# A fused feed-forward, attention and feed-forward kernel: the order of two transfers on SyncE, and four more multiplications of ones in one step of TensorE

## The reference

```python
x = x + 0.5 * ffn(layernorm(x))       # phase 0: 8 experts, capacity 512 slots each
x = x + attn(layernorm(x))            # 16 heads of 16, keys and queries normalized and rotated
x = x + 0.5 * ffn(layernorm(x))       # phase 1: 8 experts again
```

```python
scores = einsum('bhtd,bhsd->bhts', q, k) * scale + 1.0
attn = softmax(scores, axis=-1)
y = einsum('bhts,bhsd->bhtd', attn, v)
return y.reshape(B, T, C) @ wproj.T
```

## Time and profile before

| | us |
|---|---|
| three plain executions | 2152.18, 2154.19, 2148.09 |
| their median | 2152.18 |
| the profiled execution's own time | 2156.22 |
| its span, first to last instruction | 2154.3 |

### The profile page before, as it was taken

The page is one execution under the profiler, slowest core; times in us unless marked ns, Lnnn a source line. Parts: engine busy times, 40 slices in busy tenths (PEclk is TensorE's granted clock), DMA queues, the critical chain, the costliest instruction groups (busy, mean ns, idle before and its releaser), DMA issues.

```text
span 2154.3 us, 39634 instructions
## 1 busy us (share of the span) xinstructions
PE 2077.9 (96%) x14658; PEld 1073.5 (50%) x14658; DVE 1725.6 (80%) x2558; ACT 1684.0 (78%) x3255; POOL 987.9 (46%) x1221
## 2 busy tenths in 40 slices
PE   5799999999999999999999999999999999999997
PEld 4588975433444444444444444444444333236987
DVE  7776769988879888987988798888879889436774
ACT  5566647888888898988898898989888888755664
POOL 5786438652751672285067227614840201104542
PEclk9899999999999999999999999999999999899999
DMA  7454414345443444335433434435442425203331
GB/s 252 140 188 171 148 59 84 70 102 113 80 88 74 96 93 96 70 91 123 74 77 81 101 64 94 110 78 86 76 108 46 88 42 119 61 4 129 118 130 57
DMA packets 137857, 208.94 MB, mean 97 GB/s; under 512 B 30527, under 2 KB 95295, under 8 KB 137408
## 3 DMA queue, kind: packets, MB, share of 16 engines
q1 hardware_dynamic: 129792, 189.14, 36.9%
q0 software_dynamic: 7680, 16.87, 2.5%
q10 hardware_dynamic: 192, 0.39, 0.1%
HBM read 128.87 MB, written 72.01 MB: 93 GB/s over the span
## 4 chain that ended last, share of the span: by engine, by line
PE 71%; DVE 9%; issue 2%; DMA 1%; ACT 1%; SPq 1%; POOL 0%; another core or an unknown queue 0%; POOLq 0%; ACTq 0%; DVEq 0%
PE PS L1146 22%; PE PS L1129 17%; PE PS L1112 13%; PE PS L1019 6%; DVE NMX L2402 5%; PE PS L1083 3%; PE PS L826 2%; PE PS L981 1%; PE PS L983 1%; PE PS L982 1%; PE PS L961 1%; PE PS L963 1%; PE PS L962 1%; PE PS L1154 0%; DVE ST L1782 0%
## 5 line engine op out<-in xcount | busy, mean ns | idle before, releaser
L2402 DVE TENSOR_REDUCE NMX<-PS 128x1 f32<-128x1024 f32 x1024 | 1222.0, 1218 | 192.9 <-PE PS L1112 178.4
L1560 ACT ACTIVATE PB<-PS 128x512 f32<-128x512 f32 x2048 | 1104.0, 604 | 148.4 <-PE PS L1129 111.6
L1129 PE MATMUL PS<-QF,KF 51*128 51x512 f32 x2048 | 772.8, 457 | 5.5 <-ACT R L1523 2.2
L1112 PE MATMUL PS<-KF,QF 49*128 49x512 f32 x2048 | 726.4, 442 | 8.8 <-DVE NMX L2402 7.2
L1146 PE MATMUL PS<-PB,V 128*17 128x512 f32 (+1 forms) x5768 | 584.6, 477 | 0.0
L1129 PEld LDWEIGHTS PS<-QF,KF 51*128 51x128 f32 x2048 | 317.0, 185 | 419.1 <-ACT PB L1560 220.9
L1112 PEld LDWEIGHTS PS<-KF,QF 49*128 49x128 f32 x2048 | 310.5, 184 | 161.6 <-DVE NMX L2402 90.8
L1146 PEld LDWEIGHTS PS<-PB,V 128*17 128x17 f32 x5768 | 95.7, 95 | 235.6 <-issue 162.8
L2039 DVE TENSOR_TENSOR HLR<-HL,HHR 128x512 fp32r<-128x512 f32 x128 | 92.1, 720 | 87.2 <-ACT HHR L1476 79.5
L981 PE MATMUL PS<-W2H,HLR 128*128 128x256 f32 x512 | 143.0, 279 | 0.0
L983 PE MATMUL PS<-W2H,HHR 128*128 128x256 f32 x512 | 141.7, 277 | 0.0
(11 more groups left out here) (351 smaller groups left out, 3107.1 us busy)
## 6 DMA issues: line engine op xcount, KB each, us to landing
W<-in_w SPq DMA_DIRECT2D x32, 1024.0 KB
QF<-qs SPq DMA_DIRECT2D x186, 128.0 KB
KF<-qs SPq DMA_DIRECT2D x186, 128.0 KB
qs<-HI SPq DMA_DIRECT2D x64, 256.0 KB, 2.1
qs<-R1R SPq DMA_DIRECT2D x62, 256.0 KB, 2.3
QX<-x2d SPq DMA_DIRECT2D x8, 1024.0 KB, 5.4
out_x<-QX SPq DMA_DIRECT2D x8, 1024.0 KB, 5.0
YT<-YU SPq DMA_DIRECT2D x124, 64.0 KB, 3.9
```

The costliest lines, as they stand in the source:

```text
L1112: m = e.matmul(PS[:, 2 * i + half, :], QF[k][at:at + ROWS_S, p * SEQ + ti * 128:p * SEQ + ti * 128 + 128], KF[k][at:at + ROWS_S, p * SEQ + ...
L1129: e.matmul(PS[:, bank, :], KF[k][at:at + ROWS_ST, p * SEQ + sbk * 128:p * SEQ + sbk * 128 + 128], QF[k][at:at + ROWS_ST, p * SEQ + th * 51 ...
L1560: e.activation(PB[j % 3][:, h * 512:(h + 1) * 512], PS[:, place["e", tile], :], ACT.Exp).then_inc(e_out, 1)
L2402: e.tensor_reduce(NMX[:, u % 2, at:at + 1], PS[:, 2 * i:2 * i + 2, :], AX.XY, ALU.max, negate=True).then_inc(s_max, 1)
```

## The change

The value of `store` in `SOONER` goes from 65 to 67: the store of batch 6 is due in step 515 and so stands behind `load_max(31)` of step 514. And step 514 of TensorE holds five multiplications of ones where it held one.

```diff
-              65, 65, 65, 65, 66, 66, 66), scatter=(64, 65, 66, 67, 68, 69, 70, 71), store=65, load=16)
+              65, 65, 65, 65, 66, 66, 66), scatter=(64, 65, 66, 67, 68, 69, 70, 71), store=67, load=16)
...
-AGAIN = (1, 3, 18, 2, 14, 3, 9, 12, 44, 6, 28, 40, 6, 3)
+AGAIN = (1, 3, 18, 2, 14, 3, 9, 12, 44, 6, 28, 40, 6, 3, 5)
...
                 if n >= NS and j - LATE < NS and n - NS not in OUT_SEL + OUT_BEGUN + OUT_PROJ + (OUT_SEL[0] + 1,):
 
-                    again(AGAIN[0])
+                    again(AGAIN[14 if n == NS + 2 else 0])
```

## The result

Over 22 executions each the median went from 2152.55 us to 2147.28 us. The ratio of the changed kernel to the one before is 0.998, 95% interval [0.9971, 0.9989]: 0.2% faster, 2.4 to 6.2 us. The single executions of either kernel spread over some 12 us (2145.31 to 2158.0 and 2142.23 to 2154.0), more than the change is worth. The medians are 5.27 us apart. The profiled execution took 2147.51 us, its span is 2145.7 us, 8.6 us less than before.

The account below looks back on a forecast made before the run. TensorE, busy 96% of the span, was taken as the bound, slowed by waiting and a halved clock. Terms -1.10 and -4.94 us gave -6.04 from 2152.18: 2146.1 us, own range 2144 to 2148, 8-in-10 range 2143.5 to 2151.5.

Parts of the forecast that it names:

- first term (-1.10 us): TensorE, profiled execution with ScalarE's pause: step 516 starts at 1864.30 instead of 1865.40.
- second (-4.94 us): TensorE from 1865.40 to 1876.82: three steps at full clock take 6.48 us instead of 11.42.
- The order on SyncE: Loads start at 1857.66 and land at 1861.45, not 1865.35; the store, issued at about 1860.1, costs nothing.
- Rival 4: SyncE: some other wait holds the loads, leaving only the cost of ones; 2152.2 to 2153 us; chance 0.04.
- The ones: TensorE, step 514: four added products take 0.88 us, hidden in 1.58 us of idle time if ScalarE pauses.
- second branch of the working: TensorE without ScalarE's pause: ones lie open at 0.88 us, step 516 starts at 1863.04, gain 2.36 us.
- first branch: TensorE with ScalarE's pause before step 515: idle time hides the ones, step 516 starts at 1864.30, gain 1.10 us.
- The wait for the loads: TensorE before step 516: without ScalarE's pause it would have waited until 1865.35; removing that gains 2.36 us, ones included.
- The clock: TensorE's granted clock, 0.50 from 1863.0 to 1876.7, stays full after the change: -4.94 us, or 0 if it falls.
- rival 2: TensorE's clock fall is short in plain executions, costing 1.7 us; gain 2.8 us, 2149.4 us; chance 0.12.
- Rival 3: TensorE, step 514: loads were hidden anyway and the ones are not; +0.88 us, about 2153.1 us; chance 0.10.
- Rival 1: Loads are in time but TensorE's clock falls all the same; only -1.10 to -2.36 us, about 2150.5; chance 0.22.

Follow-up runs that it names:

- e1_order_only: Against the kernel before: store moved behind the four loads (store=67), one product of ones kept; ratio 0.9971 [0.9955, 0.9986], first chip.
- e9_order_only_again: Against the kernel before: again only the store moved behind the loads, one product of ones, third chip; ratio 0.998 [0.9964, 0.9995].
- e4_25_ones: Against the kernel before: store behind the loads and 25 products of ones in step 514, second chip; ratio 0.999 [0.9973, 1.0006].
- e0_before_again: The kernel before, without edit, timed and profiled a second time on the first chip; ratio 0.9997 [0.9982, 1.0011].
- e2_ones_only: Against the kernel before: five products of ones in step 514, store still ahead of the loads, first chip; ratio 0.9989 [0.9973, 1.0006].
- e5_no_ones: Against the kernel before: store behind the loads and no product of ones in step 514, second chip; ratio 0.9996 [0.9976, 1.0015].
- e8_scatters_later: Store behind the loads, one product of ones, GpSimd's batch 6 scatters held until TensorE is through step 517; ratio to the kernel before 0.9986 [0.9971, 1.0002].

## Why the prediction was right, and by which of its steps

The ratio's interval, 2.4 to 6.2 us, takes in the forecast of 6.04 us, near its end; the measured median of 2147.28 lies 1.2 us above the forecast of 2146.1. The order of the two transfers was right by its mechanism. That the total came so near is partly luck: the sum took its first term (-1.10 us) from an execution with a pause that no profile of the changed kernel has, and its second (-4.94 us) from a fall that the second profile of the kernel before has at a quarter of the length.

**The order on SyncE** was right in mechanism and size. Loads from the moment the rows are complete, the store 3.0 us behind that moment (forecast: 2.5), no wait for QF<-MT, and the later load of QX unharmed. The store cost nothing that the place shows. Rival 4, that some other wait holds the loads, is out: they started 0.03 us after the rows were complete. The experiments e1_order_only and e9_order_only_again show that the order alone brings the gain.

**The ones** were sized right: forecast 0.88 us, measured 0.87. Where there is no pause they lie open, as the second branch of the working said; it put 5.20 us between the starts of step 514 and step 516, and the profile has 5.20 (1857.15 to 1862.35). The first branch, in which the pause hides them, could not be seen in the changed kernel's profiles, none of which had a pause; e4_25_ones shows that ones lie beside such a pause. As a guard of the clock, which the forecast had made them in part, they weren't needed: it stayed at 1.00 with one product of ones as well (e1_order_only, e9_order_only_again). Whether they guard it when there is a pause stays open.

**The wait for the loads** was sized on that branch at 2.36 us with the ones, so 3.24 us without them; e0_before_again has 2.24. In the first profile the rows of maxima were complete 0.20 us before step 514 began (1857.64 and 1857.84), in the second 0.81 us before it (1854.60 and 1855.41): the sum without the pause kept a landing time that came from the execution with it.

**The clock** is the term that was mis-sized, by what it stood on. The fall of 13.70 us stands in one execution, behind a pause and not behind a wait for the loads, which was below 0.1 us there. That late loads bring a fall rests on e0_before_again alone, where 2.17 us of waiting for them is the only idling of TensorE in the place; in e2_ones_only a shorter wait had none behind it. The fall in e0_before_again is 3.4 us long, worth 1.52 us and not 4.94. That is rival 2 (the fall is short in plain executions), which had 0.12. By the second profile alone the change is worth 2.24 + 1.52 - 0.87 = 2.9 us; by the first, 7.28. The measured gain (5.3 us between the medians, 4.3 by the ratio) lies between.

How often plain executions have the long fall stays open, but the mean granted clock of each of them is on record. It is 0.9868 and 0.9873 for the kernel before on the first and third chip (35 executions each), 0.9887 for the changed kernel on both (12 each), and 0.9895 and 0.9890 for the order alone. An estimate: 0.0019 and 0.0014 of some 2150 us are 4 and 3 us of work at full clock that the changed kernel lost less. Twelve more executions of the kernel before gave 0.9878, so some 2 us of such a difference can be chance, and the mean doesn't say where in the program the clock fell. With that said, the clock's share in plain executions looks larger than the 1.52 us of the second profile and smaller than the 4.94 of the first; with 2.24 - 0.87 = 1.4 us for the wait and the ones it gives 4.4 to 5.4 us, near what was measured.

Rival 3 (slower, since the loads had been hidden and the ones are open) had its second half right and its first wrong: the wait was open. Rival 1 (in time, but the clock falls) came up in none of the three profiles of the changed kernel.

The rule of the Trainium skill, page "TensorE: Matmul & The Clock Gate", section "What's actually happening", that sustained activity releases the throttle fits the falls of 3.4 us and does not fit that of 13.70 us with TensorE busy through 13.64 us.

## What to carry to other kernels

Look through an in-order transfer queue for a large store that waits for something else ahead of small loads on the critical path: the loads pay for its wait and for its traffic too (issuing the four of them took 4.0 to 4.6 us right behind the store, and 2.6 to 3.4 us ahead of it or after it had landed). When a row shows a stall of one execution, take a second profile before a clock's fall behind it is priced. Products of ones cost nothing only where TensorE would idle, and no run here shows that they gained time there; once the wait was gone, the four added ones were a plain cost of 0.87 us, and the order alone is the better kernel by that much in the profile, if not measurably in time.

## What the runs showed of the chip that was not expected

In five profiles (the first of the kernel before and the four of the second chip) other engines got TensorE's results late while GpSimd's scatters ran or just after them: ScalarE idled for up to 3.54 us although TensorE's records of the products it needed had ended. In e4_25_ones the six exponentials that ScalarE began at 1869.46, counted back from the next pair of products (1872.60, exponential at 1873.12), belong to pairs that TensorE had started at 1864.02, 1865.26 and 1866.67. In the other nine profiles an exponential that had waited for TensorE in the place started 0.52 to 0.54 us after its pair, at full clock. It goes with the execution or the chip, not with the edits: e5_no_ones and e1_order_only differ by one product of ones, and the kernel before has it in one profile and not in the other. The scatters alone don't bring it, since they ran in the same steps in eight of the nine profiles without it. Whether they are needed for it was tried in e8_scatters_later and stays open, since that chip didn't show the pause.
